# Gated delta: the gate's second product and SiLU ahead of the first slab's transposes and squares

## The chip, the cores and the metric

The kernel runs on one core of one Trainium2 chip. A core has TensorE (PE in the profile; PEld are its weight loads), VectorE (DVE), ScalarE (ACT), GpSimd (POOL) and SyncE (SP), which here only issues DMAs. Each engine takes its own instructions in the order in which they are written; between engines they wait for each other by semaphores, which count up. The metric is the device time of one launch in microseconds, lower is better.

## What is computed

Six blocks, each added to the running x (2 x 128 tokens, width 256) after a layer norm: cross attention, the gated delta rule, a ternary-weight feed-forward, a second cross attention over 2048 tokens, a causal attention, and a mixture of experts. The change is in the second, whose core is this:

```python
def _L0_attn_ref(x, W_qkvz, W_ba, conv_w, dt_bias, A_log, norm_w, W_out):
    ...
    qkv = jax.nn.silu(conv(q | k | v))            # depthwise over time, 4 taps
    beta = sigmoid(b); g = -exp(A_log) * softplus(a + dt_bias)
    core = _chunk_gated_delta_rule(q, k, v, g, beta)
    h = core * rsqrt(mean(core * core) + EPS)     # per head, 32 heads of 128
    h = norm_w * h * jax.nn.silu(z)               # z: the gate
    return h.reshape(Bq, Sq, HV * HD) @ W_out.T
...
    # in the rule, per chunk: M is strictly lower triangular
    q = rmsnorm(q) * inv; k = rmsnorm(k) * inv
    M = where(stril, (k_beta @ k.T) * decay, 0)
    T = solve_triangular(eye + M, eye)
    v_c = T @ v_beta
    out = (q @ k.T) * decay @ v_new + ...
```

The lines are shortened here. 16 query/key heads each serve two value heads.

## The kernel before, in words

All weights and activations are float32. With 128 tokens per batch entry, the kernel treats them as one chunk. The 16 query/key heads are worked on two at a time, as a pair of *slabs* x = 0 and 1; a slab is the projection and convolution weights of one query/key head with its two value heads. There are eight pairs.

Stage b, the gated delta rule, runs a software pipeline over turns i = -2 to 7 (`TURNS`), written out by hand once for each engine (the loops `for i in TURNS` at the end of the engines' functions). In turn i an engine works on three pairs at once:

- `front`, pair j = i + 2, turns -2 to 5: projection of both slabs on TensorE (`project`, L661) into banks 0 and 1, copy into the padded buffer on ScalarE (`pads`, L900), four-tap convolution on VectorE (`conv`, L1047 and L1050, two slabs one after the other), SiLU on ScalarE (`silu`, L906). Then, slab by slab, TensorE transposes q and k of both batch entries (`squares`, L673, four transposes, into bank 0 for slab 0 and bank 1 for slab 1) and ScalarE squares them and sums along the row (`squares`, L914, four instructions, each followed by a read of its accumulator). VectorE and GpSimd make the norm factors of these sums, and TensorE multiplies keys with keys and queries (`key_products`, L685).
- `solving`, pair i, turns 0 to 7: the triangular solve. GpSimd has solved the 16 x 16 blocks; two levels double the block size with TensorE products (`diagonal_y` L750, `diagonal_z` L759), turns (`level_turn` L770), ScalarE copies (L944, L950) and masked writes by VectorE (`update`, L1106). A last level writes T's transpose, TT (`last_y` L776, `last_turn` L956 on ScalarE and L1112 on VectorE, `last_z` L783). `apply` (L791) and `attend` (L798) follow. The same pair's gate: TensorE multiplies x with the z weights of slab x into bank 2 (`gate`, L699), ScalarE writes its SiLU (`gates`, L920).
- `behind`, pair i - 1: squares, norm, gating, transposes and output projection.

The gate's product is issued twice in a turn, `gate(i, 0)` early and `gate(i, 1)` later. The second waits for its weights, for the values of pair i + 1 having been copied out of bank 2, and for the gate's SiLU before it. The transposes of `squares(j, x)` wait for ScalarE's SiLU of slab x, and the squares on ScalarE wait for these transposes. SyncE reloads the weights of slab 1's gate once `gate(i, 1)` has been multiplied; in its queue that stands behind the reload of slab 1 of the next pair, which waits for the convolution.

Nothing is scheduled by a program: the sequence of calls is the sequence on each engine.

Of the kernel before, what the change touches and what calls it, by code (L numbers as in the profile page):

```python
# [401 lines left out]
def stage_b(nc, a, env, own):  # L402
# [81 lines left out]
    def turned(x):  # L484

        return ZT[x][:, 0:2 * P].rearrange("p (v b k) -> p v b k", v=2, b=2)
# [5 lines left out]
    def has(i):  # L492
        return 0 <= i < PAIRS

    with nc.Block() as block:
# [139 lines left out]
        def _(pe):  # L635
# [9 lines left out]
            def sums():  # L645

                flat = gl[:].rearrange("p g b r -> p (g b r)")
                pe.wait_ge(gl_done, 2)
                pe.matmul(bk[5][:, 0:G_QK * U], cst[:, C_UP:C_UP + P], flat, start=True, stop=True)
                pe.matmul(bk[6][0:G_QK * U, 0:P], flat, cst[:, C_UP:C_UP + P], start=True, stop=True).then_inc(cs_mm, 1)  # L650

            def project(j, x, chunks=range(4)):
                if 0 in chunks:
                    pe.wait_ge(slab_in[x], 16 * j + 16)
                    if j or x:
                        pe.wait_ge(pads_cp, 2 * j + x)
                    if j and x == 0:
                        pe.wait_ge(sq_done, 2 * j)
                for ch in chunks:
                    for c in range(DC):  # L660
                        last = pe.matmul(PJ[ch // 2][:, ch % 2 * TOK:(ch % 2 + 1) * TOK],  # L661
                                         slab[x][:, (c * 4 + ch) * P:(c * 4 + ch + 1) * P], xnT[:, c, :],
                                         start=(c == 0), stop=(c == DC - 1))
                if 3 in chunks:
                    last.then_inc(proj_mm, 1)
# [23 lines left out]
            def gate(i, x):  # L689
                pe.wait_ge(wz_in[x], 16 * i + 16)  # L690
                if has(i + 1):
                    if x:
                        pe.wait_ge(vh_done, 2 * i + 4)
                    else:
                        pe.wait_ge(at_done, 2 * i + 3)
                pe.wait_ge(sz_done, 2 * i + x)
                for b in range(B):
                    for c in range(DC):
                        last = pe.matmul(PZ[:, b * 2 * P:(b + 1) * 2 * P], xnT[:, c, b * P:(b + 1) * P], wz[x][:, c, :],  # L699
                                         start=(c == 0), stop=(c == DC - 1))  # L700
                last.then_inc(z_mm, 1)
# [14 lines left out]
            def turn_h(i, x):  # L716
                pe.wait_ge(h_done, 2 * i + x + 1)
                for u in range(U):
                    last = pe.transpose(ZT[x][:, u * P:(u + 1) * P], hs[x][:, u, :], ident)
                last.then_inc(ht_mm, 1)  # L720
# [41 lines left out]
            def level_turn(i, k, x):  # L762

                if k == 0:
                    if i:
                        pe.wait_ge(ht_cp, 2 * (i - 1) + x + 1)
                else:
                    pe.wait_ge(t_upd, 4 * i + 2 * k)
                for v in range(2):
                    last = pe.transpose(ZT[x][:, v * P:(v + 1) * P], T[i % 2][:, x, 2 * v:2 * v + 2, :].rearrange("p u k -> p (u k)"), ident)  # L770
                last.then_inc(tr_mm, 1)
# [29 lines left out]
            for i in TURNS:  # L801
                j = i + 2
                front, value, solving, behind = has(j), has(i + 1), has(i), has(i - 1)
                if front:
                    project(j, 0)
                if i == -2:
                    sums()
                if solving:
                    gate(i, 0)
                if front:  # L810
                    project(j, 1, range(0, 2))
                if behind:
                    turn_h(i - 1, 0)
                    turn_h(i - 1, 1)
                if solving:
                    diagonal_y(i, 0, 0)
                    diagonal_y(i, 0, 1)
                    level_turn(i, 0, 0)
                    level_turn(i, 0, 1)
                if value:  # L820
                    values(i + 1, 0)
                if front:
                    project(j, 1, range(2, 4))
                if solving:
                    diagonal_z(i, 0, 0)
                    diagonal_z(i, 0, 1)
                if value:
                    values(i + 1, 1)
                if behind:
                    y_out(i - 1)  # L830
                if i == PAIRS - 2:
                    pe.wait_ge(sq_done, 2 * PAIRS)
                    for k in range(2):
                        env["w_c"]["total"](k, PJ[k])
                if solving:
                    for x in range(2):
                        diagonal_y(i, 1, x)
                        level_turn(i, 1, x)
                if front:
                    squares(j, 0)  # L840
                if solving:
                    gate(i, 1)
                    diagonal_z(i, 1, 0)
                    diagonal_z(i, 1, 1)
                if front:
                    squares(j, 1)
                    key_products(j, 1)
                if solving:
                    for x in range(2):
                        level_turn(i, 2, x)  # L850
                        last_y(i, x)
                if front:
                    key_products(j, 0)
                if solving:
                    last_z(i, 0)
                    last_z(i, 1)
                    apply(i, 0)
                    apply(i, 1)
                    attend(i, 0)
                    attend(i, 1)  # L860
# [5 lines left out]
        def _(act):  # L866
# [51 lines left out]
            def gates(i, x):  # L918
                act.wait_ge(z_mm, 2 * i + x + 1)
                act.activation(sz[i % 2][x][:].rearrange("p u k -> p (u k)"), PZ, ACT.Silu).then_inc(sz_done, 1)  # L920
# [27 lines left out]
            def level_turn(i, k, x):  # L948
                act.wait_ge(tr_mm, 2 * LEV * i + 2 * k + x + 1)
                act.copy(Tt[x][:], turned(x)).then_inc(tt_cp, 1)  # L950
# [9 lines left out]
            for i in TURNS:  # L960
                j = i + 2
                front, value, solving, behind = has(j), has(i + 1), has(i), has(i - 1)
                for x in range(2):
                    if behind:
                        outputs(i - 1, x)
                if front:
                    pads(j, 0)
                if i == -2:
                    sums()
                if solving:  # L970
                    gates(i, 0)
                    level_y(i, 0, 0)
                    level_y(i, 0, 1)
                for x in range(2):
                    if behind:
                        turn_h(i - 1, x)
                if solving:
                    level_turn(i, 0, 0)
                    level_turn(i, 0, 1)
                if i == -1:  # L980
                    decays(2)
                    decays(3)
                if value:
                    values(i + 1, 0)
                if front:
                    pads(j, 1)
                if i == PAIRS - 2:
                    env["w_c"]["sums"](0, DT[:, 0:4, :].rearrange("p g n -> p (g n)"))
                if value:
                    values(i + 1, 1)  # L990
                if front:
                    silu(j, 0)
                if i == PAIRS - 2:
                    env["w_c"]["sums"](1, DT[:, 4:8, :].rearrange("p g n -> p (g n)"))
                if solving:
                    for x in range(2):
                        level_y(i, 1, x)
                        level_turn(i, 1, x)
                if front:
                    squares(j, 0)  # L1000
                    silu(j, 1)
                if solving:
                    gates(i, 1)
                if front:
                    squares(j, 1)
                if solving:
                    last_turn(i)
                    level_y(i, 2, 0)
                    level_y(i, 2, 1)
                if i == -2:  # L1010
                    decays(0)
                    decays(1)
                if i == -1:
                    for k in range(4, PAIRS):
                        decays(k)
# [1261 lines left out]
```

## Time and profile before

| | |
|---|---|
| median of the runs shown | 883.21 us (3 runs: 881.78, 883.21, 892.46) |
| profiled execution | 887.37 us |
| its span, first to last instruction | 885.6 us |
| TensorE busy | 747.6 us (84%) |
| VectorE busy | 510.3 us (58%) |
| ScalarE busy | 373.2 us (42%) |
| GpSimd busy | 180.6 us (20%) |

A timeline row gives start, duration, engine, line of the kernel, operation, what is written and read, how many were merged into the row and, in brackets, how long the engine had been idle before it and whose result ended that. The duration of a row of TensorE holds overlapped matmuls, so neighbouring rows overlap by a tenth or two of a microsecond. The granted clock (PEclk) is TensorE's, as a share of 2.4 GHz: 0.50 is 1.2 GHz. One float32 matmul of the program shows as two records.

### The profile page before, as it was taken

To read this page: it belongs to the slowest core of one execution; us is meant where nothing else is said; L and a number is where in the kernel's file an instruction comes from. 1 tells how busy PE (TensorE), PEld (TensorE's weight loads), DVE (VectorE), ACT (ScalarE), POOL (GpSimd) and SP (SyncE) were. 2 spreads that over 40 slices of the span, in tenths; PEclk is the share of its full clock that TensorE was granted. 3 is DMA by queue.
4 is the path that set the end of the run, shared out by engine and by line. 5 is a ranking of instruction groups with operands and counts; after the bars stand their busy time and mean duration, and the time that the engine had idled before them with its cause. 6 is when DMAs were issued, how large, how long until landed. Compare 5 with 4: busy or idle time off the path is not lost. (4 is left out here: it accounts for less than half of the span.)

```text
span 885.6 us, 14636 instructions
## 1 busy us (share of the span) xinstructions
PE 747.6 (84%) x5423; PEld 565.9 (64%) x5424; DVE 510.3 (58%) x1250; ACT 373.2 (42%) x1020; POOL 180.6 (20%) x363
## 2 busy tenths in 40 slices
PE   5856558999999988772479999999999989886998
PEld 3744446887887867560347667666767777664655
DVE  1536665769878873533536665566666425663561
ACT  1504874456456445223225545545555423221220
POOL 1012883156545633000000000000000010000000
PEclk9657868999999999775569999999999999996999
DMA  5003212633133112000393111110201034000000
GB/s 195 1 0 137 109 53 81 226 106 101 28 93 104 22 46 59 24 1 0 113 287 65 22 39 21 26 34 20 40 20 13 7 104 188 1 1 0 1 0 13
DMA packets 44454, 53.21 MB, mean 60 GB/s; under 512 B 29120, under 2 KB 34368, under 8 KB 43136
## 3 DMA queue, kind: packets, MB, share of 16 engines
q1 hardware_dynamic: 43104, 50.16, 18.5%
q0 software_dynamic: 1280, 2.12, 2.3%
q8 instruction: 44, 0.72, 0.4%
q14 instruction: 26, 0.21, 0.1%
HBM read 50.90 MB, written 1.36 MB: 59 GB/s over the span
## 5 line engine op out<-in xcount | busy, mean ns | idle before, releaser
L1606 ACT COPY d_Pt<-bank 128x512 f32<-128x512 f32 x96 | 51.6, 589 | 102.2 <-PE bank L1529 102.2
L1681 DVE TENSOR_REDUCE d_nm<-scores 128x1 f32<-128x1024 f32 x64 | 75.4, 1219 | 20.4 <-PE scores L1522 20.4
L1050 DVE SCALAR_TENSOR_TENSOR b_yc<-b_cpad,b_slab,b_yc 128x256 f32<-128x256 f32 x192 | 79.9, 488 | 0.0
L1618 ACT ACTIVATE d_Pr<-scores,d_negm 128x1024 f32<-128x1024 f32 x64 | 70.7, 1109 | 17.7 <-DVE d_negm L1684 17.7
L1529 PEld LDWEIGHTS bank<-cst,d_Pr 128*128 128x128 f32 x512 | 56.2, 141 | 29.1 <-issue 24.7
L1529 PE MATMUL bank<-cst,d_Pr 128*128 128x128 f32 x512 | 69.2, 278 | 0.4 <-DVE d_Pt L1658 0.4
L1522 PE MATMUL scores<-d_KM,d_Q 64*128 64x512 f32 x256 | 65.4, 630 | 2.0 <-ACT d_Q L1597 2.0
L661 PE MATMUL bank<-xnT,b_slab 128*128 128x256 f32 x256 | 63.9, 401 | 2.1 <-ACT b_cpad L900 2.1
L1542 PE MATMUL bank<-d_Pt,d_KV 128*64 128x128 f32 x1024 | 63.0, 276 | 0.0
L1542 PEld LDWEIGHTS bank<-d_Pt,d_KV 128*64 128x64 f32 x1024 | 55.2, 137 | 7.8 <-issue 5.8
L661 PEld LDWEIGHTS bank<-xnT,b_slab 128*128 128x128 f32 x256 | 51.4, 206 | 10.3 <-issue 2.7
L1455 POOL DMA_DIRECT2D d_spread<-d_rc x16 | 8.9, 556 | 208.0 <-DVE d_rc L1648 208.0
L1658 DVE COPY d_Pt<-bank 128x512 f32<-128x512 f32 x32 | 20.6, 686 | 37.2 <-PE bank L1529 37.2
L699 PE MATMUL bank<-b_wz,xnT 128*128 128x256 f32 x128 | 32.3, 397 | 7.7 <-issue 7.7
L1522 PEld LDWEIGHTS scores<-d_KM,d_Q 64*128 64x128 f32 x256 | 22.5, 190 | 25.3 <-issue 21.0
L605 POOL TENSOR_TENSOR b_S<-b_S,b_tmp 64x14 f32<-64x14 f32 (+6 forms) x112 | 33.7, 301 | 8.8
L603 POOL TENSOR_TENSOR b_tmp<-b_G,b_S 64x14 f32<-64x14 f32 (+6 forms) x112 | 33.5, 299 | 8.7
L733 PE MATMUL bank<-b_wo,b_hT 128*128 128x256 f32 x128 | 33.0, 416 | 0.8 <-ACT b_hT L933 0.8
L938 ACT ACTIVATE b_yc<-scores 128x128 f32<-128x128 f32 x64 | 16.7, 290 | 39.1 <-PE scores L798 39.1
L699 PEld LDWEIGHTS bank<-b_wz,xnT 128*128 128x128 f32 x128 | 24.5, 199 | 11.7 <-issue 8.6
L944 ACT COPY b_Ys<-scores 128x256 f32<-128x256 f32 x32 | 11.4, 373 | 48.2 <-PE scores L750 48.1
L584 POOL TENSOR_TENSOR b_hr<-b_hv,mhalf 128x4 f32<-128x4 f32 x16 | 15.9, 1008 | 73.6 <-DVE b_hv L1128 73.5
(327 smaller groups left out, 1551.1 us busy)
## 6 DMA issues: line engine op xcount, KB each, us to landing
b_slab<-in_b_slab SPq DMA_DIRECT2D x16, 520.0 KB, 3.7
b_wz<-in_b_wz SPq DMA_DIRECT2D x16, 256.0 KB, 3.7
b_wo<-in_b_wo SPq DMA_DIRECT2D x16, 256.0 KB, 2.9
d_w<-in_d_w SPq DMA_DIRECT2D x16, 224.0 KB, 2.5
b_DT<-b_cs SPq DMA_DIRECT2D x2, 1536.0 KB, 10.4
f_w<-in_f_w SPq DMA_DIRECT2D x3, 896.0 KB, 10.0
c_w<-in_c_w SPq DMA_DIRECT2D x2, 1024.0 KB, 6.2
d_wo<-in_d_wo SPq DMA_DIRECT2D x1, 2048.0 KB, 8.2
```

Of the source, the lines that this page charges most:

```text
L603: plink(pool.tensor_tensor(t, G[:, m, m + 1:W].unsqueeze(2).to_broadcast([PROBLEMS, n, m]), S[:, m, 0:m].unsqueeze(1).to_broadcast([PROBLE ...
L605: last = pool.tensor_tensor(S[:, m + 1:W, 0:m], S[:, m + 1:W, 0:m], t, ALU.add)
L661: last = pe.matmul(PJ[ch // 2][:, ch % 2 * TOK:(ch % 2 + 1) * TOK], slab[x][:, (c * 4 + ch) * P:(c * 4 + ch + 1) * P], xnT[:, c, :], start ...
L699: last = pe.matmul(PZ[:, b * 2 * P:(b + 1) * 2 * P], xnT[:, c, b * P:(b + 1) * P], wz[x][:, c, :], start=(c == 0), stop=(c == DC - 1))
L733: last = pe.matmul(PY[:, b * D:(b + 1) * D], hT[x][:, b * RATIO + r, :], wo[x][:, r, :], start=(x + r == 0), stop=(x + r == 2))
L1050: last = dve.scalar_tensor_tensor(yc[x][:, ch], src, tap, yc[x][:, ch], ALU.mult, ALU.add)
L1522: pe.matmul(scores[:, 2 * k + half, :], Q[h % 2][rows, tok], KM[b][rows, keys], start=True, stop=True).then_inc(done, 1)
L1529: last = pe.transpose(TP[g % 2][:, j * P:(j + 1) * P], Pr[m % 2][:, (4 * g + j) * P:(4 * g + j + 1) * P], ident)
L1542: last = pe.matmul(CT[half * LAT:(half + 1) * LAT, q], KV[:, b, 4 * k + j, half, :], Pt[2 * k + half][:, j, :], start=(k + j == 0), stop=( ...
L1606: act.copy(Pt[g][:].rearrange("p j q -> p (j q)"), TP[g % 2]).then_inc(pt_cp[g % 2], 1)
L1618: act.activation(Pr[b][:, keys], scores[:, 2 * k:2 * k + 2, :].rearrange("p g k -> p (g k)"), ACT.Exp, bias=negm[:, b:b + 1], accum_out=su ...
L1681: last = dve.tensor_reduce(nm2[:, b, k:k + 1], scores[:, 2 * k:2 * k + 2, :].rearrange("p g k -> p (g k)"), AX, ALU.max, negate=True)
```

## The change

In the turns 0 to 5, in which an engine has both a front pair and a solving pair, the second gate product moves on TensorE from behind to ahead of slab 0's transposes, and its SiLU on ScalarE from behind slab 1's SiLU to ahead of slab 0's squares. In turns 6 and 7 there is no front pair, and the calls come in the same sequence as before. No operation, buffer or semaphore is added or taken away.

```diff
@@ TensorE @@
                 for x in range(2):
                     diagonal_y(i, 1, x)
                     level_turn(i, 1, x)
+            if solving:
+                gate(i, 1)
             if front:
                 squares(j, 0)
             if solving:
-                gate(i, 1)
                 diagonal_z(i, 1, 0)
                 diagonal_z(i, 1, 1)
@@ ScalarE @@
                 for x in range(2):
                     level_y(i, 1, x)
                     level_turn(i, 1, x)
+            if solving:
+                gates(i, 1)
             if front:
                 squares(j, 0)
                 silu(j, 1)
-            if solving:
-                gates(i, 1)
-            if front:
                 squares(j, 1)
             if solving:
                 last_turn(i)
```

TensorE in a turn, from the second level's products (L750) to the key products (L685). Before:

```order
L750 MATMUL scores<-b_T,b_Np 64x64 x8
L770 MATMUL scores<-cst,b_T 128x128 x2
L673 MATMUL bank<-cst,b_qkv 128x128 x4
L699 MATMUL bank<-b_wz,xnT 128x256 x4
L759 MATMUL scores<-b_Ys,b_Tt 64x64 x16
L673 MATMUL bank<-cst,b_qkv 128x128 x4
L685 MATMUL bank<-b_qkv 128x256 x2
```

After:

```order
L750 MATMUL scores<-b_T,b_Np 64x64 x8
L770 MATMUL scores<-cst,b_T 128x128 x2
L699 MATMUL bank<-b_wz,xnT 128x256 x4
L673 MATMUL bank<-cst,b_qkv 128x128 x4
L759 MATMUL scores<-b_Ys,b_Tt 64x64 x16
L673 MATMUL bank<-cst,b_qkv 128x128 x4
L685 MATMUL bank<-b_qkv 128x256 x2
```

The four products of the gate (L699) and the first four transposes (L673) have changed places; L759 and the second four transposes stand where they stood.

ScalarE in the same place, from the last copies of the second level (L944, L950) to the squares of slab 1. Before:

```order
L944 COPY b_Ys<-scores 128x256
L950 COPY b_Tt<-scores 128x256
L914 ACTIVATE b_yc,b_ssq<-bank 128x128 x4
L906 ACTIVATE b_qkv<-b_yc 128x1024
L920 ACTIVATE b_sz<-bank 128x512
L914 ACTIVATE b_yc,b_ssq<-bank 128x128 x4
```

With the change each line number is one higher (L921 is the gate's SiLU, L915 the squares, L907 the SiLU of a slab):

```order
L945 COPY b_Ys<-scores 128x256
L951 COPY b_Tt<-scores 128x256
L921 ACTIVATE b_sz<-bank 128x512
L915 ACTIVATE b_yc,b_ssq<-bank 128x128 x4
L907 ACTIVATE b_qkv<-b_yc 128x1024
L915 ACTIVATE b_yc,b_ssq<-bank 128x128 x4
```

The gate's SiLU now stands ahead of slab 0's squares and of slab 1's SiLU; the squares of slab 1 follow slab 1's SiLU directly.

## Rows read from the trace of the kernel before

**Rows 1.** The page, its table of engines: busy us (share of the span), instructions.
```profile
PE 747.6 (84%) x5423; PEld 565.9 (64%) x5424; DVE 510.3 (58%) x1250; ACT 373.2 (42%) x1020; POOL 180.6 (20%) x363
```

**Rows 2.** Busy time by stretches (columns in the first line), turns 1 to 5 together.
```profile
core 0: us, PE busy (x) PEld busy (x) DVE busy (x) ACT busy (x) POOL busy (x), PEclk, DMA share, GB/s
163.17:325.50 162.33, 155.55 (x1502) 131.61 (x1500) 133.48 (x407) 85.52 (x302) 85.58 (x186) 1.00 0.32 95
```

**Rows 3.** Timeline of TensorE, turn 4: start us, us, engine, line, op, out<-in, count [idle].
```profile
280.65 0.60 PE L673 MATMUL bank<-cst,b_qkv 128*128 128x128 f32 x4
281.09 1.89 PE L699 MATMUL bank<-b_wz,xnT 128*128 128x256 f32 x8
282.91 0.98 PE L759 MATMUL scores<-b_Ys,b_Tt 64*64 64x64 f32 x32
283.82 0.66 PE L673 MATMUL bank<-cst,b_qkv 128*128 128x128 f32 x4
...
288.12 1.14 PE L783 MATMUL scores<-b_TT,b_Ys 64*64 64x64 f32 x16
```

**Rows 4.** Timeline of ScalarE, turn 4.
```profile
282.51 1.06 ACT L906 ACTIVATE b_qkv<-b_yc 128x1024 f32<-128x1024 f32 x1
283.47 0.58 ACT L920 ACTIVATE b_sz<-bank 128x512 f32<-128x512 f32 x1
284.51 0.28 ACT L914 ACTIVATE b_yc<-bank 128x128 f32<-128x128 f32 x1 [0.46 <-PE bank L673]
```

**Rows 5.** Timeline of TensorE, first and second L673 of turns 1 and 2.
```profile
183.02 0.60 PE L673 MATMUL bank<-cst,b_qkv 128*128 128x128 f32 x4
...
186.18 0.65 PE L673 MATMUL bank<-cst,b_qkv 128*128 128x128 f32 x4
...
215.92 0.60 PE L673 MATMUL bank<-cst,b_qkv 128*128 128x128 f32 x4
...
219.15 0.63 PE L673 MATMUL bank<-cst,b_qkv 128*128 128x128 f32 x4
```

**Rows 6.** Timeline of ScalarE, turn 1: first square and next SiLU.
```profile
183.66 0.28 ACT L914 ACTIVATE b_yc<-bank 128x128 f32<-128x128 f32 x1
...
184.67 1.07 ACT L906 ACTIVATE b_qkv<-b_yc 128x1024 f32<-128x1024 f32 x1
```

**Rows 7.** Timeline of turn 0, where slab 1's SiLU ends a wait.
```profile
151.10 1.06 ACT L906 ACTIVATE b_qkv<-b_yc 128x1024 f32<-128x1024 f32 x1 [2.21 <-DVE b_yc L1050]
...
152.30 0.63 PE L673 MATMUL bank<-cst,b_qkv 128*128 128x128 f32 x4 [2.12 <-ACT b_qkv L906]
...
158.14 1.14 PE L783 MATMUL scores<-b_TT,b_Ys 64*64 64x64 f32 x16
```

**Rows 8.** Timeline of turn 4: VectorE, then SyncE's queue.
```profile
277.51 4.96 DVE L1050 SCALAR_TENSOR_TENSOR b_yc<-b_cpad,b_slab,b_yc 128x256 f32<-128x256 f32 x12
...
286.57 1.20 DVE L1112 COPY b_TT<-scores 64x128 f32<-64x128 f32 x4 [2.13 <-PE scores L770]
...
288.16 3.64 SPq L523 DMA_DIRECT2D b_T<-b_solved  x8
```

**Rows 9.** Timeline of TensorE: three idle times and what ended them.
```profile
138.05 0.98 PE L750 MATMUL scores<-b_T,b_Np 64*64 64x64 f32 x32 [1.60 <-DMA b_T<-b_solved]
...
270.73 1.01 PE L770 MATMUL scores<-cst,b_T 128*128 128x128 f32 x4 [1.06 <-ACT b_hT L933]
...
328.72 1.53 PE L699 MATMUL bank<-b_wz,xnT 128*128 128x256 f32 x6 [3.05 <-issue]
```

**Rows 10.** Busy time by stretches, with TensorE's granted clock, behind those idle times.
```profile
139.25:142.50 3.25, 3.25 (x13) 2.87 (x12) 0.00 (x0) 1.78 (x5) 0.00 (x0) 0.50 0.10 11
...
152.85:156.25 3.40, 3.40 (x16) 2.47 (x15) 0.00 (x0) 2.27 (x13) 1.44 (x7) 0.50 0.54 203
...
328.70:340.00 11.30, 9.39 (x105) 7.61 (x106) 3.76 (x16) 7.16 (x14) 5.23 (x18) 1.00 0.17 38
...
270.70:280.00 9.30, 9.13 (x94) 7.42 (x96) 9.30 (x26) 5.43 (x12) 7.42 (x24) 1.00 0.20 61
```

## The prediction

> **What bounds the kernel now.** I first read the table of engines on the page: TensorE has matmuls in flight for 84% of the span [rows 1]. Then the busy time by stretches. The change touches the loop of the gated delta stage, which makes ten turns (i = -2 to 7). Turns 1 to 5 take 162.33 us together, 32.5 each, and TensorE is busy for 155.55 of them, at the full clock; VectorE has 133.48, ScalarE only 85.52 [rows 2]. Such busy time counts overlapped matmuls in full, so it does not by itself say that TensorE has nothing to spare. The order of events does, and for that I read TensorE's timeline of turn 4: from 280.65 to 288.12 no row names an idle time, and each begins where the one before ends or slightly earlier [rows 3]. Whatever stops TensorE there is paid in full unless a wait further on takes it up.
>
> ScalarE has time to spare in total, but in this place it works in TensorE's interest: the two play one chain back and forth. TensorE transposes slab 0's query and key (L673, first row), ScalarE squares them (L914), then SiLU makes slab 1's values (L906), and the second L673, 3.17 us after the first, cannot begin before that. The gate's SiLU (L920) comes behind L906 at 283.47, and behind it ScalarE still waits 0.46 us for TensorE [rows 3, 4]. So the gate's SiLU fills a hole on ScalarE now and costs nothing.
>
> **The change part by part.**
>
> *TensorE, the gate's four matmuls (eight records in the trace; products below) ahead of the first four transposes.* The same instructions, the other way round. The transposes begin 0.44 us before the products (280.65, 281.09) and the products 1.82 us before L759 (282.91) [rows 3]. After: products at 280.65, transposes at 280.65 + 1.82 = 282.47, L759 at 282.91 as before. Nothing for TensorE itself, and the second VectorE update of T, which waits for L759, stays where it is. The products need bank 2 free, which the value copies gave back microseconds earlier; VectorE, GpSimd and SyncE keep their order. The reload of the gate's weights waits for these products, but SyncE reaches it only behind the slab load that waits for the convolution, so it leaves no earlier.
>
> *ScalarE, the gate's SiLU ahead of the squares.* This is what costs. ScalarE starts 0.04 us after TensorE's result (transposes 183.02 + 0.60, squares 183.66 [rows 5, 6]). For turn 4:
> - products end at 280.65 + 1.89 = 282.54; the gate's SiLU starts at 282.58;
> - it takes 0.58 us and the next instruction starts 0.10 us before its end (as 283.47 stands to 282.51 + 1.06 [rows 4]): 283.06. The transposes end at 282.47 + 0.60 = 283.07, so the squares start at 283.11;
> - the four squares with their reads take 1.01 us to the next instruction (183.66 to 184.67, a turn in which ScalarE did not wait there [rows 6]): slab 1's SiLU starts at 284.12, ends after 1.06 us at 285.18;
> - TensorE follows 0.14 us after a SiLU that it waits for (151.10 + 1.06 = 152.16, start 152.30 [rows 7]): second L673 at 285.32.
>
> It was at 283.82: **1.50 us later**, with TensorE idle for 285.32 - 283.89 = 1.43 us behind L759. Put as a spacing, first transposes to second go from 3.17 to 4.67 us. In turn 1 the spacing is 3.16 and in turn 2 it is 3.23 [rows 5], which gives 1.51 and 1.44; turns 3 and 5 have turn 4's to 0.01. Sum over turns 1 to 5: 1.51 + 1.44 + 3 x 1.50 = **7.5 us**.
>
> *Turn 0* is different: there TensorE already waits 2.12 us for the SiLU of slab 1, and that SiLU waits 2.21 us for VectorE's convolution [rows 7]. The gate's SiLU fits in front of it. Cost 0; if the convolution came earlier it would be the 1.5 of the other turns. Turns 6 and 7 have no slabs to transform, and there the order is the old one: 0.
>
> *Does something later take the 1.5 us up?* Everything behind the second L673 hangs on it in program order: key products, the last level, ScalarE's and VectorE's copies to TT (VectorE waits 2.13 us for TensorE there [rows 8]), the last solve products at 288.12 [rows 3]. The values, the weighting by VectorE, the norm, the keys and the convolutions of the next turn come behind these, each relative to the one before. VectorE's convolution of slab 1 is back to back until 277.51 + 4.96 = 282.47 [rows 8], but it starts in the next turn as much later as TensorE does, so it does not open a slack. The blocks that GpSimd solved are written back by SyncE from 288.16 for 3.64 us [rows 8] and read in the next turn behind its projections and the gate's first product; a slip of the turn only adds to that. I take up nothing; the bounds are 0 (all taken up) and 1.5 per turn.
>
> *The granted clock.* The new idle time can have a price of its own. In this stage the clock went to 0.50 (1.2 GHz) for over 3 us behind idle times of 1.60 and 2.12 us [rows 7, 9, 10]. It stayed at 1.00 behind one of 1.06 and one of 3.05 us [rows 9, 10]. The new one, 1.43, lies between these, next to 1.60. What a fall costs in just this place is in turn 0: second L673 to L783 takes 158.14 - 152.30 = 5.84 us [rows 7] against 288.12 - 283.82 = 4.30 at the full clock [rows 3]: 1.54. Bounds: none falls, 0; all five fall, 7.7. Of three idle times of at least 1.5 us that these rows hold, two had a fall; ours is a little shorter, so I take two falls of five, **3.1 us**.
>
> On this the Trainium skill (TensorE: Matmul & The Clock Gate, Why this matters for your kernels) warns only of gaps of more than about 3 us between bursts. By it no turn would fall and the sum would be 7.5 alone. The trace disagrees in both directions: shorter gaps than that had a fall behind them and one of 3.05 us had none [rows 7, 9, 10], so I keep my own count.
>
> **Sum.** 7.5 + 3.1 = 10.6 us. The profiled execution took 887.37 us, so it would give 898.0. That execution is 4.2 us above the median of the runs shown, 883.21, and the forecast is made on the median: **893.8 us**, 1.2% slower. About 2% (17.7 us) is what a measurement of this kernel can tell from no change, so I forecast "slower, within 2%".
>
> **The rivals.**
>
> *Free of cost.* ScalarE's chain is late anyway, because slab 1's SiLU waits for VectorE, as in turn 0. It decides if the convolution ends at least 1.6 us later against the first L673 than the 282.47 of turn 4 (new SiLU start 284.12). For it: turn 0, and the SiLU in turn 4 starts just as the convolution ends. Against it: VectorE's work hangs on the same chain and slips with it, so the distance stays. It gives 883.2, not slower than now.
>
> *The clock never falls.* 7.5 alone: 890.7.
>
> *The clock falls in four or five turns.* 7.5 + 7.7 = 898.4. For it: a fall behind 1.60 us; TensorE's work on both sides of the new gap is small products and transposes, as around the 2.12 us of turn 0. Against it: turns that start at another point fare differently, as the 3.05 us without a fall shows.
>
> *Slower by over 2%.* The slow stretch is twice as long in each turn, as if the gap of 1.06 us before L770 held it there: 5 x 2 x 1.54 + 7.5 = 22.9, or 906.1. No turn shows that, so it gets little.
>
> *The change does nothing.* The gate would have to be issued at the old place; both engines' orders show that it is not, in six turns.
>
> **How the numbers follow.** One to three falls 0.45 (890.7 + 1.54 to + 4.6, my forecast in the middle at two); no fall 0.25; four or five 0.15; free, wholly or mostly, 0.09; over 2% 0.06. The range takes in the first three, 890.7 to 898.4. It is widened below by 4 us, since the runs shown have a fastest 1.4 us under the median and part of the delay may be taken up, and above by 2: **886.5 to 900.5**. Faster by over 2% 0.02 (no mechanism here; only disturbed times would do it), slower by over 2% 0.08 (the last rival and the upper edge of the one before), within 2% 0.90.
>
> **What the new profile would show.** TensorE: in turns 1 to 5 an idle time of about 1.4 us before the second four transposes, released by the SiLU of slab 1, and 4.7 us between first and second transposes; turns of 34.0 us at the full clock and 35.5 where it fell. ScalarE: no wait left between slab 0's squares and slab 1's SiLU, a wait for TensorE of about 0.7 us before slab 1's squares (0.46 now). Turn 0 as now, and L759 still right behind TensorE's work. The mechanism is wrong if the second transposes have no idle time before them, or if they have it and the turns still take 32.4 us; the clock's term is wrong if all gaps, or none, are followed by a granted clock of 0.50.

## The result

| | before | changed |
|---|---|---|
| median, 20 runs each | 888.02 us (881.78 to 892.46) | 893.88 us (887.83 to 899.72) |
| ratio of medians of the runs compared | | 1.0066, interval 1.0044 to 1.0087 |
| profiled execution, its span | 887.37, 885.6 us | 895.28, 893.5 us |

The changed kernel is slower by 0.66%, 5.9 us (3.9 to 7.7), less than the 2% that a verdict goes by. The forecast time of 893.8 us stands beside a measured 893.88, but that closeness is luck: more runs put the kernel before at 888.0, not 883.2. The forecast difference, 10.6 us, is too large by 4.7. Every ratio leaves out runs more than 1.5% above the fastest of their kernel, which is one of all: the profiled one with two copies more.

The profile after. Busy time by stretches first, turns 1 to 5 one by one and together (columns as in [rows 2]):

```profile
164.25:198.05 33.80, 31.10 (x303) 26.41 (x301) 24.18 (x83) 17.02 (x62) 14.99 (x34) 1.00 0.55 194
198.05:231.85 33.80, 31.10 (x303) 26.42 (x302) 27.27 (x83) 17.02 (x62) 17.84 (x38) 1.00 0.27 73
231.85:265.64 33.79, 31.09 (x302) 26.40 (x301) 27.24 (x82) 17.00 (x62) 17.83 (x38) 1.00 0.27 73
265.64:299.44 33.80, 31.10 (x302) 26.42 (x301) 27.26 (x82) 17.02 (x62) 17.54 (x38) 1.00 0.25 71
299.44:333.24 33.80, 31.10 (x302) 26.39 (x300) 27.25 (x82) 17.02 (x62) 17.53 (x38) 1.00 0.16 40
164.25:333.24 168.99, 155.48 (x1502) 132.04 (x1500) 133.20 (x406) 85.08 (x302) 85.73 (x186) 1.00 0.30 90
```

Turns 1 to 5 take 168.99 us where they took 162.33 [rows 2]: 6.66 us longer, with TensorE busy for the same 155.5 us and the granted clock at 1.00 throughout. So all of it is idle time of TensorE, and the list of TensorE's waits in these turns says which (engine, line and what was waited for: us in total, times, longest):

```profile
PE bank L673 <- ACT b_qkv L907: 7.1, 5, 1.4
PE scores L770 <- ACT b_hT L934: 5.3, 5, 1.1
```

The wait for L934 is old, L933 in [rows 9]. The wait for L907, the SiLU of a slab, is new, five times 1.41 us. Turn 4 on TensorE's timeline, to be laid beside [rows 3]:

```profile
285.48 1.89 PE L699 MATMUL bank<-b_wz,xnT 128*128 128x256 f32 x8
287.21 0.60 PE L673 MATMUL bank<-cst,b_qkv 128*128 128x128 f32 x4
287.74 0.98 PE L759 MATMUL scores<-b_Ys,b_Tt 64*64 64x64 f32 x32
290.13 0.63 PE L673 MATMUL bank<-cst,b_qkv 128*128 128x128 f32 x4 [1.41 <-ACT b_qkv L907]
```

The gate's products (L699) come first, the transposes 1.73 us later, L759 right behind, and then TensorE stands. From the front of this group, now the gate's products, to the second transposes it is 290.13 - 285.48 = 4.65 us, where it was 3.17 from the transposes that stood in front. ScalarE in the same turn, against [rows 4]:

```profile
287.41 0.60 ACT L921 ACTIVATE b_sz<-bank 128x512 f32<-128x512 f32 x1 [1.36 <-PE bank L699]
287.91 0.27 ACT L915 ACTIVATE b_yc<-bank 128x128 f32<-128x128 f32 x1
...
288.90 1.08 ACT L907 ACTIVATE b_qkv<-b_yc 128x1024 f32<-128x1024 f32 x1
290.80 0.28 ACT L915 ACTIVATE b_yc<-bank 128x128 f32<-128x128 f32 x1 [0.81 <-PE bank L673]
```

ScalarE waits 1.36 us for the gate's products, runs SiLU, four squares and slab 1's SiLU without a wait, and then waits 0.81 us for the second transposes. No granted clock of 0.50 follows any of the five gaps. The page has the clock in 40 slices of 22.3 us each, in tenths; turns 1 to 5 lie in slices 8 to 15, and all their digits are 9, the highest:

```profile
PEclk9657868999999999686559999999999999996999
```

### The profile page after: what moved, and what is told of

It reads as the page before. It is cut to its first block and busy times, and to the rows that moved or that the text cites. A ratio compares the mean times of both kernels' runs of the same rounds, so it can differ in the third digit from the quotient of the medians.

```text
span 893.5 us, 14636 instructions
## 1 busy us (share of the span) xinstructions
PE 749.9 (84%) x5423; PEld 568.0 (64%) x5424; DVE 510.0 (57%) x1250; ACT 372.7 (42%) x1020; POOL 180.2 (20%) x363
## 3 DMA queue, kind: packets, MB, share of 16 engines
HBM read 50.90 MB, written 1.36 MB: 58 GB/s over the span
## 5 line engine op out<-in xcount | busy, mean ns | idle before, releaser
L1050 DVE SCALAR_TENSOR_TENSOR b_yc<-b_cpad,b_slab,b_yc 128x256 f32<-128x256 f32 x192 | 79.4, 485 | 0.0
L699 PE MATMUL bank<-b_wz,xnT 128*128 128x256 f32 x128 | 32.2, 397 | 7.3 <-issue 7.3
L673 PE MATMUL bank<-cst,b_qkv 128*128 128x128 f32 x64 | 11.8, 316 | 28.2 <-ACT b_qkv L907 28.2
L699 PEld LDWEIGHTS bank<-b_wz,xnT 128*128 128x128 f32 x128 | 24.5, 199 | 10.9 <-issue 7.8
## 6 DMA issues: line engine op xcount, KB each, us to landing
b_DT<-b_cs SPq DMA_DIRECT2D x2, 1536.0 KB, 10.7
```

The costliest lines, as they stand in the source:

```text
L1050: last = dve.scalar_tensor_tensor(yc[x][:, ch], src, tap, yc[x][:, ch], ALU.mult, ALU.add)
```

## The experiments

The kernels ran in three groups, each group on one chip beside the kernel before, and each ratio is against the kernel before of its group: the first four sections are one group, turn0_only to h_first the second, the rest the third. "Spacing" below means from the first of the two operations (slab 0's transposes or the gate's products) to slab 1's transposes, in turns 1 to 5.

### TensorE's half alone (pe_only)

```diff
+                if solving:
+                    gate(i, 1)
                 if front:
                     squares(j, 0)
                 if solving:
-                    gate(i, 1)
                     diagonal_z(i, 1, 0)
```

> Only TensorE's half of the change: the gate's second product ahead of the first four transposes; ScalarE keeps the old order. Theory A (the delay is the transposes waiting behind the gate's 1.82 us of products): the squares start 1.82 us later, slab 1's SiLU no longer waits for the convolution and starts 1.4 to 1.5 us later than before, the second transposes too; five turns, about +7 us (+0.8%), the same as the whole change. Theory B (the delay is the gate's SiLU standing ahead of slab 1's SiLU on ScalarE, as the prediction's heading has it): less than half of that, under +3.5 us.

Measured: 1.0066 (1.0046 to 1.0085), the whole change's ratio. TensorE's timeline in turn 4:

```profile
285.99 0.60 PE L673 MATMUL bank<-cst,b_qkv 128*128 128x128 f32 x4
...
288.86 0.63 PE L673 MATMUL bank<-cst,b_qkv 128*128 128x128 f32 x4 [1.36 <-ACT b_qkv L907]
```

1.36 us idle, against 1.41 with both halves. Theory A holds: it is the transposes behind the gate's products that delay slab 1's SiLU. With the whole change, ScalarE's SiLU of the gate lies almost wholly inside the time in which ScalarE has to wait for these transposes anyway: a turn takes 33.80 us with it there and 33.75 in this kernel.

### ScalarE's half alone (act_only)

```diff
+                if solving:
+                    gates(i, 1)
                 if front:
                     squares(j, 0)
                     silu(j, 1)
-                if solving:
-                    gates(i, 1)
-                if front:
                     squares(j, 1)
```

> Only ScalarE's half: the gate's SiLU ahead of slab 0's squares; TensorE keeps the old order, so the product that this SiLU waits for ends at 282.98 in turn 4's times. ScalarE then stands still until 283.02, the squares follow at 283.50, slab 1's SiLU at 284.51, the second transposes at 285.71: +1.9 us a turn, +9.4 us (+1.1%) over five turns, more than the whole change. If instead the moves of the two engines add up (each a part of the 1.45), it gives under +5 us.

Measured: 1.0099 (1.0068 to 1.0131), +8.8 us. Same view, turn 4:

```profile
286.26 0.60 PE L673 MATMUL bank<-cst,b_qkv 128*128 128x128 f32 x4
...
291.35 0.63 PE L673 MATMUL bank<-cst,b_qkv 128*128 128x128 f32 x4 [1.85 <-ACT b_qkv L906]
```

Idle 1.85 us, spacing 291.35 - 286.26 = 5.09, that is +1.92 where 1.9 was expected. The halves do not add up: either alone costs as much as both or more. With TensorE's half slab 1's SiLU comes late because the transposes do, with ScalarE's half because ScalarE stands until the gate's products, still behind the transposes, have ended.

### Slab 1's SiLU ahead of slab 0's squares (silu_first)

```diff
 # on the changed kernel, ScalarE
                 if front:
-                    squares(j, 0)
                     silu(j, 1)
+                    squares(j, 0)
                     squares(j, 1)
```

> The whole change, and on ScalarE slab 1's SiLU also ahead of slab 0's squares: gate's SiLU, SiLU, squares, squares. If the delay goes to TensorE through slab 1's SiLU alone, the idle time before the second transposes falls from 1.41 us to about 0.3 to 0.5 us (the SiLU starts at 283.06, ends at 284.12, transposes at 284.26), and the kernel is 2 to 3 us slower than before. If the squares of slab 0 also are waited for (norm, next turn), it stays near +7 us.

Measured: 1.0014 (0.9988 to 1.0040), not to be told from no change; its median is 4.9 us below that of the changed kernel on the same chip (889.27, 894.21). Its trace has turns of 32.77 us, 0.42 more than the kernel before, about 2 us in five turns.

```profile
282.82 0.60 PE L673 MATMUL bank<-cst,b_qkv 128*128 128x128 f32 x4
...
284.71 0.63 PE L673 MATMUL bank<-cst,b_qkv 128*128 128x128 f32 x4 [0.38 <-ACT b_qkv L907]
```

The idle time has shrunk from 1.41 to 0.38 us. So the path runs through slab 1's SiLU alone; the squares of slab 0 may come about 1 us later without harm.

### The changed kernel again

> The changed kernel once more, on the same chip as the three above, with a second profile. Expected +6 to +8 us against the kernel before, idle 1.41 us in five turns. Whether the clock falls behind these gaps: my forecast had two falls of five, the first profile has none; if the falls depend on where a turn happens to lie, one of the profiles of this group shows some.

Measured: 1.0069 (1.0044 to 1.0094). Five more gaps of 1.41 to 1.42 us, again none with a fall behind it: from the second L673 to L783 each turn took 4.28 or 4.29 us, the full-clock value of [rows 3] (4.30). The mean granted clock of this kernel's seven runs was 0.902, that of the kernel before on the same chip 0.899 in 24 runs; runs with falls have 0.885 to 0.891 (below, one copy more). So it is not that my profiles missed the falls. The forecast of two falls is wrong.

### The change in turn 0 alone (turn0_only)

```diff
 # TensorE, and ScalarE likewise
+                if i == 0:
+                    gate(i, 1)
                 if front:
                     squares(j, 0)
                 if solving:
-                    gate(i, 1)
+                    if i:
+                        gate(i, 1)
```

> The change in turn 0 alone, the old order in turns 1 to 5. By the prediction this is free, since slab 1's SiLU waits for VectorE's convolution there: ratio 1.000, spacing of the L673s 5.4 us less the 1.8 by which the first comes later, second L673 where it was. If the moved product costs TensorE's time in every turn, as in turns 1 to 5, it gives +1.4 us here.

Measured: 0.9989 (0.9968 to 1.0009): free, as forecast. The first L673 comes 2.00 us behind the transposes of L770 before it, where it was 0.36, so 1.6 us later; the wait for slab 1's SiLU stays (2.40 us).

### One and two copies more on ScalarE (dose1, dose2)

```diff
 # on the changed kernel, ScalarE; idle is a tile of its own
                     squares(j, 0)
+                    if i > 0:
+                        for k in range(1):        # 2 in the second kernel
+                            act.copy(idle[:, k, :], cst[:, 0:C_LV])
                     silu(j, 1)
```

> The changed kernel with one more ScalarE copy (128x512, to a tile of its own that nobody reads) ahead of slab 1's SiLU in turns 1 to 5. If ScalarE's chain from the gate's product to slab 1's SiLU is on the path one for one, the idle time grows from 1.41 to about 1.9 us and the kernel by 2.5 us over the changed one (+8.5 us against before). If later waits took part of the 1.41 up, the growth per turn is not the same as that of the idle time. If the clock falls behind gaps of this size, each fall adds 1.5 us.

> As the one before with two copies: idle about 2.4 us in turns 1 to 5, +11 us against before at the full clock. Turn 0 has had an idle time of 2.1 to 2.4 us with a fall of the clock behind it in every profile so far; if that size is enough, all five turns fall here and the kernel is +19 us; if it takes more than the size, none or some fall.

Measured with one copy: 1.0178 (1.0131 to 1.0224), 895.38 us in the profiled execution. TensorE in turn 4, then L784 (L783 before) in the same turn:

```profile
285.11 0.60 PE L674 MATMUL bank<-cst,b_qkv 128*128 128x128 f32 x4
...
288.55 0.63 PE L674 MATMUL bank<-cst,b_qkv 128*128 128x128 f32 x4 [1.93 <-ACT b_qkv L908]
...
292.83 1.14 PE L784 MATMUL scores<-b_TT,b_Ys 64*64 64x64 f32 x16
```

The idle time is 1.93 us and turns take 34.32 against 33.80: +0.52 us for +0.52 of idle time, one for one. In this execution no turn fell (4.28 us from second transposes to L784). Two of the six runs were of this kind, 894.5 and 895.4 us at a mean clock of 0.902 and 0.901; the other four took 902.9 to 907.2 at 0.885 to 0.891. Those four are 7.5 to 12.8 us longer than these two. At 1.54 us a fall, the price in turn 0, that is about five falls or more, though the gaps had grown by half a microsecond only. There is no trace of the four: that they had falls is read from their time and clock, and which turns fell is not known.

Two copies: 1.0260 (1.0223 to 1.0298). The profile is of the longest run (921.86 us, 5.5 us above the next), so only its pattern is read. Busy time by stretches, from each second group of transposes to L784 in turns 1 to 5:

```profile
189.11:195.71 6.60, 6.60 (x33) 4.72 (x33) 1.23 (x5) 2.92 (x14) 5.30 (x16) 0.60 0.05 14
228.41:234.15 5.74, 5.74 (x33) 4.31 (x33) 1.23 (x5) 2.92 (x14) 0.21 (x1) 0.74 0.17 25
264.71:271.80 7.09, 7.09 (x33) 4.97 (x33) 1.23 (x5) 2.92 (x14) 1.59 (x1) 0.56 0.11 12
305.49:312.42 6.93, 6.93 (x33) 4.87 (x33) 1.23 (x5) 2.92 (x14) 1.59 (x1) 0.57 0.12 12
344.80:352.66 7.86, 7.86 (x32) 5.67 (x32) 1.23 (x5) 2.92 (x14) 1.58 (x1) 0.50 0.10 10
```

Behind gaps of 2.45 us all five turns have a lowered clock (0.50 to 0.74 on average) and take 5.74 to 7.86 us where 4.28 is the full-clock time. The delay by itself makes 5 x (1.45 + 1.04) = 12.5 us; the other five runs took 19.6 to 28.8 over the median of the kernel before, at a mean clock of 0.884 to 0.891. The 7 to 16 us between are again about five falls or more, so falls are no peculiarity of the profiled run, but only its trace shows them turn by turn.

### The heads' copy first (h_first)

```diff
 # on the kernel before, ScalarE
                     gates(i, 0)
-                    level_y(i, 0, 0)
-                    level_y(i, 0, 1)
                 for x in range(2):
                     if behind:
                         turn_h(i - 1, x)
                 if solving:
+                    level_y(i, 0, 0)
+                    level_y(i, 0, 1)
                     level_turn(i, 0, 0)
```

> The kernel before, with one other edit: in a turn ScalarE copies the turned heads (L933) ahead of the first level's products (L944), so that TensorE no longer waits 1.06 us for L933 before L770. Theory: TensorE's idle time is the bound, and five to seven turns give back 1.06 us each, 5 to 7 us (-0.7%). Rival: the loop is as much VectorE's, which is back to back until slab 1's convolution ends at 282.47 in turn 4, and slab 1's SiLU begins 0.04 us later; then TensorE only comes earlier to a wait and the gain is 0.1 us a turn, ratio 1.000.

Measured: 0.9956 (0.9941 to 0.9971), -3.9 us: between the two theories. TensorE's waits in the loop say why:

```profile
PE bank L673 <- ACT b_qkv L906: 5.6, 4, 1.5
PE bank L699 <- issue: 3.4, 2, 3.1
```

The wait for L933 is gone, and in four turns a wait for slab 1's SiLU has come in its place. Turn 1 takes 31.45 us from first transposes to first transposes where it took 32.90, turns 3 and 4 take 32.28 and 32.26 against 32.35. From turn 0's first transposes to turn 1's it is 34.66 us where it was 36.10. So the theory is right for these two stretches (1.44 and 1.45 us off, more than the wait of 1.06 itself) and the rival for the later ones. The rest of the gain is in turns 6 and 7, where there is no convolution and the kernel before has this wait twice more:

```profile
PE scores L770 <- ACT b_hT L933: 2.1, 2, 1.1
```

It is gone from the same list of h_first.

### The change where slab 1's SiLU waits for the convolution (h_first_after)

The changed kernel with the same edit.

> The changed kernel with the heads' copy (L933) first, the edit of h_first. In h_first slab 1's SiLU waits for VectorE's convolution in turns 2 to 5 (TensorE idle 1.36 to 1.50 us before the second transposes) and not in turn 1. If the change costs nothing where that SiLU waits for the convolution anyway, it costs here only in turn 1: h_first plus 1.5 to 2 us, about 2 us faster than before (ratio 0.998). If it costs 1.45 us in every turn whatever the convolution does, it is h_first plus 7, ratio 1.004.

Measured: 0.9969 (0.9949 to 0.9990), h_first plus 1.2 us. In turns 2 to 5 ScalarE's chain and VectorE's convolution now end within tenths of a microsecond of each other, and a turn takes 32.31 us where h_first has 32.26. Turns 1 and 2 on TensorE:

```profile
183.20 0.60 PE L673 MATMUL bank<-cst,b_qkv 128*128 128x128 f32 x4
...
186.12 0.63 PE L673 MATMUL bank<-cst,b_qkv 128*128 128x128 f32 x4 [1.42 <-ACT b_qkv L907]
...
215.51 0.60 PE L673 MATMUL bank<-cst,b_qkv 128*128 128x128 f32 x4
...
218.43 0.63 PE L673 MATMUL bank<-cst,b_qkv 128*128 128x128 f32 x4 [1.42 <-ACT b_qkv L907]
```

First transposes to first transposes, 215.51 - 183.20, are those 32.31 us. So the same two moves that cost 1.45 us a turn in the kernel before cost next to nothing once the convolution ends late enough. That is the rival "free of cost", under the condition that I had given for it: in h_first the convolution of turn 4 ends 3.36 us behind the first L673 (280.75, 277.39), in the kernel before 1.82 (282.47, 280.65), so 1.54 us later where I had asked for 1.6.

### GpSimd's four operations behind the solve (lat_late)

Why the convolution ends late in turns 2 to 5 but not in turn 1 is visible on VectorE: its first taps, L1047, four instructions each, in turn 4 of the kernel before:

```profile
267.29 3.32 DVE L1047 TENSOR_SCALAR b_yc<-b_cpad,b_slab 128x256 f32<-128x256 f32 x4
```

beside them on GpSimd:

```profile
266.96 1.27 POOL L1380 TENSOR_TENSOR d_raw<-d_raw,d_rope 128x512 f32<-128x512 f32 x1
268.31 1.27 POOL L1381 TENSOR_TENSOR d_KV<-d_raw,d_swapped 128x512 f32<-128x512 f32 x1
```

```diff
 # on the kernel before, GpSimd
-                if 1 < i < 6:
-                    env["w_d"]["rotate_latents"](i - 2)
                 early = 8 if i == -1 else W - 1
                 if has(i + 1):
                     solve(i + 1, range(1, early))
+                if 1 < i < 6:
+                    env["w_d"]["rotate_latents"](i - 2)
```

> The kernel before, with GpSimd's four large operations for the later stage (L1378 to L1381) behind the solve instead of ahead of it in turns 2 to 5. In turn 4 VectorE's first taps (L1047, 4 instructions) took 3.32 us while two of these ran, and 1.14 in turn 1 of h_first. Theory: the two engines hinder each other; with GpSimd's part moved L1047 takes 1.1 to 1.2 us for four and the convolutions end some 2 us earlier, but TensorE is the bound in this order and the kernel gains 0 to 1 us. Rival: the length of L1047 has another cause; it stays above 3 us.

Measured: 1.0011 (0.9987 to 1.0034), no gain. VectorE in turn 4:

```profile
264.44 1.13 DVE L1047 TENSOR_SCALAR b_yc<-b_cpad,b_slab 128x256 f32<-128x256 f32 x4
```

3.32 us have become 1.13, so GpSimd's work does hinder VectorE. TensorE has no use for it in this order: turns 3 and 4 take 32.35 us as before, with no wait for slab 1's SiLU in either kernel.

### Both edits, with and without the change (h_lat, h_lat_after)

> Both edits, the heads' copy first and GpSimd's four operations late. If h_first's gain was cut short in turns 2 to 5 by the convolution's end, it now comes in all turns: turns of about 30.9 us, 5 x 1.4 us off, 7 to 9 us faster than before (ratio 0.990 to 0.992). If not, it stays at h_first's 0.996.

> The change on top of both edits. The convolution is early again, so the change should cost its 1.45 us in each of turns 1 to 5: h_lat plus 7 us. If it stays free as in the turns in which SiLU waits for the convolution, it equals h_lat.

Measured: both edits 0.9880 (0.9850 to 0.9911), 877.34 us, 10.7 us faster than before and better than either edit's gain added to the other's (0.9956 and 1.0011). With the change on top 0.9964 (0.9944 to 0.9984): the change costs 0.84% there, 7.2 us between the medians, against 7.3 for five turns at 1.45. TensorE in turn 4 of both, first without and then with the change:

```profile
244.38 0.60 PE L673 MATMUL bank<-cst,b_qkv 128*128 128x128 f32 x4
...
275.24 0.60 PE L673 MATMUL bank<-cst,b_qkv 128*128 128x128 f32 x4
...
278.40 0.66 PE L673 MATMUL bank<-cst,b_qkv 128*128 128x128 f32 x4
```

```profile
281.59 0.60 PE L673 MATMUL bank<-cst,b_qkv 128*128 128x128 f32 x4
...
284.51 0.63 PE L673 MATMUL bank<-cst,b_qkv 128*128 128x128 f32 x4 [1.42 <-ACT b_qkv L907]
```

A turn without the change takes 30.86 us (275.24 - 244.38), with it 32.31.

## Why the prediction was right or wrong

**The delay of slab 1's SiLU: right.** The working gave 1.50 us later, 1.43 idle and a spacing of 4.67; the trace shows 1.41 idle and 4.65. The prediction calls the 4.67 the spacing from first to second transposes, and this is wrong by its own times: it is the one from the gate's products. The transposes themselves were due at 282.47 and 285.32, 2.85 us apart, and are 2.92 apart (287.21, 290.13). Turns of 34.0 us were expected and 33.80 came: I had added the 1.50 to the mean of the five turns, 32.5, which holds the extra time between turns 1 and 2 (see below); against the 32.35 of an ordinary turn it is 1.45.

**"ScalarE ... This is what costs": wrong in its place.** I put the cost on the gate's SiLU ahead of the squares. My own two numbers, squares free to start at 283.06 and transposes ended at 283.07, were a tie, and I read only one side. TensorE's half alone costs the same 0.66%, so with both moves the SiLU of the gate adds almost nothing, 0.05 us a turn.

**"I take up nothing": nearly right.** Five turns at 1.45 make 7.3, but the turns together grew by 6.66. The rest is in the kernel before: from the first L673 of turn 1 to that of turn 2 it takes 32.90 us [rows 5], and to the later ones 32.38 and 32.35. At the end of turn 1 VectorE waits there for GpSimd's power of the norm. Both rows in the kernel before, and then in the changed one:

```profile
193.42 1.64 POOL L578 TENSOR_TENSOR b_r<-b_m,mhalf 128x8 f32<-128x8 f32 x1
195.09 0.16 DVE L1061 TENSOR_TENSOR b_r<-b_r 128x4 f32<-128x4 f32 x1 [0.62 <-POOL b_r L578]
```

```profile
194.49 1.64 POOL L578 TENSOR_TENSOR b_r<-b_m,mhalf 128x8 f32<-128x8 f32 x1
196.92 0.15 DVE L1061 TENSOR_TENSOR b_r<-b_r 128x4 f32<-128x4 f32 x1
```

In the changed kernel GpSimd's power comes 1.07 us later, and VectorE comes to its row 2.45 us later than it would have without the wait (195.09 - 0.62 = 194.47). GpSimd has 1.4 us more, and the wait is gone. So 0.6 us of one turn's delay were taken up; I had looked for such a wait in turn 4 alone.

**Turn 0 and turns 6 and 7 free: right**, by the run with the change in turn 0 only.

**The clock, 3.1 us for two falls: wrong.** This is the step that made 10.6 of 7.5. Ten gaps of 1.4 us in two profiles of the changed kernel, five of 1.36, five of 1.85 and five of 1.93 us in the experiments have no fall behind them. Five of 2.45 all have one, in one profile. The gap of 1.93 us is not safe for all that: four of the six executions with it have the time and the clock of about five falls or more. I had counted three idle times from one trace, at different places of the program, as if their size told the chance. That one trace showed one fall behind 1.60 us [rows 9, 10], whose gap began 0.7 us after an earlier stretch at 0.50, and none in the steady turns. The earlier stretch:

```profile
130.00:135.70 5.70, 5.70 (x14) 4.53 (x15) 4.77 (x15) 3.14 (x6) 0.67 (x2) 0.50 0.13 21
```

By the Trainium skill's rule that I set aside (TensorE: Matmul & The Clock Gate, Why this matters for your kernels) no fall was due, and the sum without the term, 7.5, lies inside the measured 3.9 to 7.7. But the rule alone would have failed for gaps of 2.45 us, which are shorter than the 3 us that it names, as are the 12 gaps of 2.1 to 2.4 us in turn 0 with a fall behind them.

**The rivals.** "The clock never falls" is what happened, 0.25 where I had given 0.45 to one to three falls. "Free of cost" is a real state of this loop, shown in turns 2 to 5 of h_first_after, but not of this kernel. "Four or five falls" needs longer gaps: half a microsecond more was enough in four executions of six, by their time and clock, and a microsecond more in the profiled one with two copies.

## What to carry to other kernels

An operation that fills a hole on one engine can be moved only as far as the hole goes: before moving it, ask what the operations that it now stands ahead of release on the other engine, and write down both ends of a tie. Where two engines bound a loop together, speeding up one alone shows little (-0.4% and nothing here) and both together much (-1.2%). The price of an idle time in clock is to be read from gaps at the same place in the loop, and from more than one execution: with one copy more, two executions of the same kernel showed nothing of a fall in time or clock, and four were 7.5 to 12.8 us longer.

## What was not expected of the hardware

GpSimd's elementwise work hinders VectorE where both have their operands in SBUF: four L1047 take 3.32 us beside it and 1.13 without. It goes the other way round too. In lat_late GpSimd's copy L598 falls beside VectorE's later taps (L1050), and in turn 4 it takes 3.74 us where it took 0.67, first in the kernel before and then in lat_late:

```profile
269.52 0.67 POOL L598 COPY b_S<-b_G 64x256 f32<-64x256 f32 x1
```

```profile
267.05 3.74 POOL L598 COPY b_S<-b_G 64x256 f32<-64x256 f32 x1 [4.06 <-DMA b_G<-b_blocks]
```

The Trainium skill (SBUF — State Buffer, SBUF: two separate sides) says that the two engines share a pair of ports, which an instruction of GpSimd, or one of VectorE in a mode with two ports or (against an instruction of GpSimd that reads SBUF) with two inputs in SBUF, holds from its start to its end while the other engine is blocked. L1050 has two such inputs. No view shows the mode of L1047, so its rows agree with the page as far as they go.

Whether the clock falls behind a long gap is not a matter of its size alone. Turn 0 has a gap of 2.1 to 2.4 us in each of the 14 profiles, before and changed included; in 12 the stretch behind it took 5.8 to 5.9 us, as in [rows 7], and in two 4.3. TensorE in turn 0 of the kernel with one copy, one of the two:

```profile
151.25 0.63 PE L674 MATMUL bank<-cst,b_qkv 128*128 128x128 f32 x4 [2.32 <-ACT b_qkv L908]
...
155.53 1.14 PE L784 MATMUL scores<-b_TT,b_Ys 64*64 64x64 f32 x16
```

2.32 us idle and then 155.53 - 151.25 = 4.28 us, the full-clock time. What decides between the two is left open.
